# Attention and mixture-of-experts layer on one core: table load, expert parts, projections and plan moved within the steps

## The reference

```python
def attn(x, Wq, bq, Wk, bk, Wv, bv, Wo, bo):        # x: (8, 256, 256), 16 heads of 16
    q, k, v = x @ Wq.T + bq, x @ Wk.T + bk, x @ Wv.T + bv
    phi_q, phi_k = elu(q) + 1, elu(k) + 1
    kv_sum = cumsum(phi_k * v, axis=1)              # along the 256 rows, elementwise
    return (phi_q * kv_sum) * 0.25 @ Wo.T + bo

def ffn(x, router_w, w1, w2, w_gate, w_up, w_down):  # 2048 tokens, 8 experts, top 2
    top, idx = top_k(x @ router_w, 2)
    scores = softmax(top)
    routed = sum over the two experts e of a token:
             score * ((silu(x @ w1[e][:, :512]) * (x @ w1[e][:, 512:])) @ w2[e])
    shared = (silu(x @ w_gate) * (x @ w_up)) @ w_down
    return routed + shared

x = x + attn(layernorm(x), ...)
x = x + ffn(layernorm(x), ...)
```

## Time and profile before

| | before |
|---|---|
| median of 3 runs | 377.15 us (376.57 to 378.16) |
| profiled execution, its own time | 377.39 us |
| its span, first to last instruction | 375.7 us |
| PE busy | 340.8 us (91%) |
| DVE, ACT, POOL busy | 235.5, 214.5, 189.3 us |
| granted TensorE clock, mean | 0.976 |

### The profile page before, as it was taken

The page is one execution under the profiler, slowest core; times in us unless marked ns, Lnnn a source line. Parts: engine busy times, 40 slices in busy tenths (PEclk is TensorE's granted clock), DMA queues, the critical chain, the costliest instruction groups (busy, mean ns, idle before and its releaser), DMA issues.

```text
span 375.7 us, 9015 instructions
## 1 busy us (share of the span) xinstructions
PE 340.8 (91%) x2868; PEld 252.9 (67%) x2868; DVE 235.5 (63%) x579; ACT 214.5 (57%) x385; POOL 189.3 (50%) x293
## 2 busy tenths in 40 slices
PE   7866599999997999999999899999999999999980
PEld 6655488787786878878888555655566566656660
DVE  5977976687766886798677655464544533443430
ACT  3767639666775686876526345544545545455440
POOL 4823085578586775937134532453353534434432
PEclk9998989999998999999999999999999999999995
DMA  7976052337355462464845826647475676695530
GB/s 194 384 190 201 15 130 64 76 91 227 56 149 191 106 198 67 115 199 142 253 154 164 159 54 100 96 70 109 76 111 85 100 101 87 97 109 88 84 49 0
DMA packets 77467, 46.41 MB, mean 124 GB/s; under 512 B 61040, under 2 KB 72560, under 8 KB 77040
## 3 DMA queue, kind: packets, MB, share of 16 engines
q1 hardware_dynamic: 63088, 35.08, 37.0%
q0 software_dynamic: 9664, 10.71, 17.6%
q10 hardware_dynamic: 4672, 0.07, 0.9%
HBM read 19.09 MB, written 12.97 MB: 85 GB/s over the span
## 4 chain that ended last, share of the span: by engine, by line
PE 46%; POOL 18%; DVE 10%; issue 9%; DMA 7%; ACT 7%; POOLq 1%; SPq 1%; DVEq 0%; ACTq 0%
PE bU L1027 13%; PE bG L1027 12%; PE bV L1048 6%; POOL x_rows L570 6%; PE bQ L1048 6%; DMA xs<-bo 3%; PE bK L1007 2%; DMA xT<-rows 2%; PE bU L237 2%; PE bG L237 2%; DVE ab L1475 1%; DMA stage<-in_w_expert 1%; DVE st L1352 1%; POOL y L510 1%; POOL nt L517 1%
## 5 line engine op out<-in xcount | busy, mean ns | idle before, releaser
L1475 DVE SCALAR_TENSOR_TENSOR ab<-bU,sg 128x512 f32<-128x512 f32 x64 | 44.1, 689 | 77.0 <-PE bU L1027 52.2
L761 POOL DMA_INDIRECT out_y<-xs,dst_row x32 | 50.0, 1562 | 60.2 <-DMA out_y<-xs,dst_row 39.2
L1158 ACT ACTIVATE sg<-bG 128x512 f32<-128x512 f32 x64 | 37.9, 593 | 45.4 <-PE bG L1027 26.6
L1027 PE MATMUL bG<-we,work 128*128 (+1 forms) x216 | 52.6, 380 | 1.7 <-DVE wd L1531 1.7
L1027 PE MATMUL bU<-we,work 128*128 (+1 forms) x216 | 52.6, 379 | 0.0
L1302 ACT ACTIVATE ws_h<-ab 128x512 f16<-128x512 f32 x36 | 22.7, 629 | 41.6 <-DVE ab L1475 40.1
L570 POOL DMA_INDIRECT x_rows<-rows,slot_u x32 | 35.1, 1098 | 21.3 <-DVE slot_u L1526 10.7
L1751 DVE TENSOR_TENSOR ws_h<-ab,ws_h 128x512 f16<-128x512 f32 x36 | 25.0, 694 | 20.7 <-ACT ws_h L1302 20.7
L1165 ACT ACTIVATE ah<-ab 128x512 f16<-128x512 f32 x32 | 20.1, 628 | 26.9 <-DVE ab L1475 26.8
L1027 PEld LDWEIGHTS bG<-we,work 128*128 128x128 f16 (+1 forms) x216 | 20.7, 99 | 21.2 <-issue 3.6
L1027 PEld LDWEIGHTS bU<-we,work 128*128 128x128 f16 (+1 forms) x216 | 19.8, 99 | 17.4
(11 more groups left out here) (321 smaller groups left out, 813.8 us busy)
## 6 DMA issues: line engine op xcount, KB each, us to landing
stage<-in_w_expert SPq DMA_DIRECT2D x24, 512.0 KB, 4.6
we<-in_w_shared SPq DMA_DIRECT2D x3, 1024.0 KB, 10.7
xs<-bo POOLq DMA_DIRECT2D x8, 256.0 KB, 3.9
out_y<-xs SPq DMA_DIRECT2D x8, 256.0 KB, 2.5
xs<-in_x SPq DMA_DIRECT2D x1, 1280.0 KB, 19.7
x_rows<-we SPq DMA_DIRECT2D x9, 134.0 KB, 2.4
xs<-in_x SPq DMA_DIRECT2D x3, 256.0 KB, 4.3
work<-x_rows SPq DMA_TRANSPOSE x40, 3.2
```

The lines of the kernel that those rows point to most:

```text
L761: pool.indirect_dma_start(out_rows, bass.IndirectOffsetOnAxis(ap=dst_row[:, b:b + 1], axis=0), ya[b % NY], None, bounds_check=NT * P - 1, ...
L1027: ins = pe.matmul(dst[t * n:(t + 1) * n, :], x2[:, hi * KC + k, t * n:(t + 1) * n], w[t][lo][:, k, half, :], start=s == 0 and k == 0, stop ...
L1158: act.activation(sg[q][:], src[:], ACT.Silu, scale=1.0 / WS).then_inc(S["sg_done"], 1)
L1475: dve.scalar_tensor_tensor(out=ab[q][:], in0=src[:], scalar=1.0 / WS, in1=sg[q][:], op0=ALU.mult, op1=ALU.mult).then_inc(S["a_done"], 1)
```

## The change

All of it is order; besides that, four tiny Exp activations are added.

- **ACT, table.** In steps 3 to 6 a new `load_exp()` (an Exp of one number for each partition, into `spare`) stands behind `silu(n + 3, 1)`, so that the compiler's load of the Exp table stands there and no longer at the head of the next step. `act_hi(j, 3)` goes ahead of `normed2(i)`.
- **ACT and DVE, expert parts.** On ACT the first part of a step goes behind `silu(n, 0)`, the others each one place forward. On DVE steps 3, 5 and 6 take their three parts at the places that steps 4 and 7 already used for their first three (the first one ahead of `swiglu(n + 2, 0)`), and only steps 4 and 7 have one at the end.
- **DVE, second norm.** `logits(i - 1, 2)` goes ahead of `stats2(i)`, `moments2(i)` ahead of `act_lo(j, 1)`.
- **PE.** In steps 3 to 7 Q is projected second and V third. In the last batches `down(B - 2, 0)` goes ahead of `route(B - 1)`, and `spread_plan()` ahead of `gate_up(B - 1, 3)`.
- **Last batches.** Part (B, 2) goes ahead of the plan, the others forward by one place; SP loads part 22 ahead of the clearing of rows; DVE copies the plan's table ahead of part (B, 5); POOL makes the masks ahead of its wait for the token numbers; for block 0 `placed` goes behind `routed_act_lo`.

```diff
 # SP
             load_part(20)
             load_part(21)
+            load_part(22)
...
-            load_part(22)
             load_part(23)
 # PE
-                project(i)
+                project(i, "kqv")
...
             gate_up(B - 2, 1)
+            down(B - 2, 0)
             route(B - 1)
             gate_up(B - 2, 2)
-            down(B - 2, 0)
...
             down(B - 1, 0)
+            spread_plan()
             gate_up(B - 1, 3)
 # ACT
+            def load_exp():
+                act.activation(spare[:], bias[:, 0, 0:1], ACT.Exp)
...
+                first = 0 if i in FOUR else 1
                 exps(i)
                 silu(n, 0)
+                expert_hi(part_of_step(i, first))
                 context_hi(i)
...
                 act_hi(j, 1)
-                if i in FOUR:
-                    expert_hi(part_of_step(i, 0))
-                expert_hi(part_of_step(i, 1))
+                expert_hi(part_of_step(i, first + 1))
                 choice(i - 1)
-                if i not in FOUR:
-                    expert_hi(part_of_step(i, 2))
+                expert_hi(part_of_step(i, first + 2))
                 silu(n + 2, 0)
-                if i in FOUR:
-                    expert_hi(part_of_step(i, 2))
                 act_hi(j, 2)
                 silu(n + 3, 1)
+                if i < B - 1:
+                    load_exp()
+                act_hi(j, 3)
                 normed2(i)
-                act_hi(j, 3)
                 row_hi2(i)
-                expert_hi(part_of_step(i, 3))
+                if i in FOUR:
+                    expert_hi(part_of_step(i, 3))
 # DVE
                 residual(i)
+                logits(i - 1, 2)
                 stats2(i)
-                logits(i - 1, 2)
+                moments2(i)
                 act_lo(j, 1)
-                moments2(i)
                 if ahead:
                     row_lo(0, i + 1)
-                if i in FOUR:
-                    expert_lo(part_of_step(i, 0))
+                first = 0 if i in FOUR else 1
+                expert_lo(part_of_step(i, first))
                 swiglu(n + 2, 0)
-                expert_lo(part_of_step(i, 1))
+                expert_lo(part_of_step(i, first + 1))
                 slots(i - 1, 0)
                 act_lo(j, 2)
                 slots(i - 1, 1)
                 swiglu(n + 3, 1)
-                expert_lo(part_of_step(i, 2))
+                expert_lo(part_of_step(i, first + 2))
                 act_lo(j, 3)
                 row_lo(1, i)
-                expert_lo(part_of_step(i, 3))
+                if i in FOUR:
+                    expert_lo(part_of_step(i, 3))
...
             act_lo(j, 2)
+            expert_lo(part_of_step(B, 2))
             swiglu(n + 3, 1, bV)
```

More of the change, by code:

```diff
@@ L107, in layer_kernel @@
         row_f = sb("row_f", [P, 1])
+        spare = sb("spare", [P, 1])
         xs = sb("xs", [P, NT, D])
@@ L697, in _ @@
                 pool.dma_start(meta[:, b, :], xrows[bass.ds(at, P), 2 * D:2 * D + 8]).then_inc(S[f"first_meta{b}"], 16)
+            pool.wait_ge(S["spread_out"], 2)
+            pool.tensor_copy(pad_i[:, 0:NBLK], past[:, 0:NBLK]).then_inc(S["pad_done"], 1)
+            for t in range(2):
+                then(pool.tensor_scalar(half_pad[:, :, t], mixed_of(past), other[:, t:t + 1], None, ALU.max), wait=t == 1)
+            pool.tensor_copy(half_pad_i[:], half_pad[:]).then_inc(S["pad_done"], 1)
+            then(pool.tensor_tensor(pad_f[:, 1:NBLK], bexp_c[:, 1:NBLK], bexp_c[:, 0:NBLK - 1], ALU.subtract))
+            then(pool.tensor_scalar(pad_f[:, 1:NBLK], pad_f[:, 1:NBLK], 0.0, 16.0, ALU.is_gt, ALU.mult))
             pool.wait_ge(S["spread_in"], 2)
@@ L707, in _ @@
             pool.tensor_scalar(ends[:, 1, :], pick_block[:], tok_f[:, 1:2], None, ALU.mult).then_inc(S["ends_in"], 1)
-            pool.wait_ge(S["spread_out"], 2)
-            pool.tensor_copy(pad_i[:, 0:NBLK], past[:, 0:NBLK]).then_inc(S["pad_done"], 1)
-            for t in range(2):
-                then(pool.tensor_scalar(half_pad[:, :, t], mixed_of(past), other[:, t:t + 1], None, ALU.max), wait=t == 1)
-            pool.tensor_copy(half_pad_i[:], half_pad[:]).then_inc(S["pad_done"], 1)
-            then(pool.tensor_tensor(pad_f[:, 1:NBLK], bexp_c[:, 1:NBLK], bexp_c[:, 0:NBLK - 1], ALU.subtract))
-            then(pool.tensor_scalar(pad_f[:, 1:NBLK], pad_f[:, 1:NBLK], 0.0, 16.0, ALU.is_gt, ALU.mult))
             pool.wait_ge(S["ends_out"], 1)
@@ L792, in project @@
                     pe.wait_ge(S["xT1_in"], 16 * TB * (i - 2))
-                for m, name, done, free in ((0, "k", "k_ps", "rk_done"), (1, "v", "v_ps", "kv_done"), (2, "q", "q_ps", "rq_done")):
-                    if name not in which:
-                        continue
+                parts = {"k": (0, "k_ps", "rk_done"), "v": (1, "v_ps", "kv_done"), "q": (2, "q_ps", "rq_done")}
+                for name in which:
+                    m, done, free = parts[name]
                     if i >= 2:
@@ L1059, in expert @@
                 return pe.snap(expert_reg[b % 3], min_val=0, max_val=E - 1)
-            spread_plan()
             pe.wait_ge(S["bexp_done"], 1)
@@ L1277, in _ @@
             act_hi(j, 2)
+            expert_hi(part_of_step(B, 2))
             silu(n + 3, 1, bK)
@@ L1282, in _ @@
             silu(n, 0)
+            expert_hi(part_of_step(B, 3))
             act_hi(j, 0)
-            expert_hi(part_of_step(B, 2))
             silu(n + 1, 1, bK)
             act_hi(j, 1)
-            expert_hi(part_of_step(B, 3))
+            expert_hi(part_of_step(B, 4))
             silu(n + 2, 0)
-            expert_hi(part_of_step(B, 4))
+            expert_hi(part_of_step(B, 5))
             act_hi(j, 2)
             silu(n + 3, 1, bK)
-            expert_hi(part_of_step(B, 5))
             act_hi(j, 3)
@@ L1733, in _ @@
             act_lo(j, 0)
-            expert_lo(part_of_step(B, 2))
+            expert_lo(part_of_step(B, 3))
             swiglu(n + 1, 1, bV)
             act_lo(j, 1)
-            expert_lo(part_of_step(B, 3))
+            expert_lo(part_of_step(B, 4))
             shared_out(B - 2)
             swiglu(n + 2, 0)
-            expert_lo(part_of_step(B, 4))
+            dve.wait_ge(S["spread_ps"], 1)
+            dve.tensor_copy(bexp_c[:, 0:NBLK], bR[:, 0:NBLK]).then_inc(S["spread_out"], 1)
+            dve.tensor_scalar(past[:, 0:NBLK], bR[:, NBLK:2 * NBLK], row128[:], float(BIG), ALU.is_le, ALU.mult).then_inc(S["spread_out"], 1)
+            expert_lo(part_of_step(B, 5))
             act_lo(j, 2)
             swiglu(n + 3, 1, bV)
-            expert_lo(part_of_step(B, 5))
             act_lo(j, 3)
@@ L1755, in placed @@
                 if k == 0:
+                    if b == 0:
+                        dve.wait_ge(S["spread_out"], 2)
+                        dve.wait_ge(S["pad_done"], 2)
                     dve.wait_ge(*meta_in(b))
@@ L1797, in _ @@
             for b in range(NBLK):
-                placed(b, 0)
+                if b >= 1:
+                    placed(b, 0)
                 swiglu(NP * B + b, b % 2)
-                placed(b, 1)
+                if b >= 1:
+                    placed(b, 1)
                 routed_act_lo(b)
+                if b == 0:
+                    placed(b, 0)
+                    placed(b, 1)
                 if b == 1:
```

5 lines of the change are left out of this document (removed).

## The result

Over six executions each, taken in turn on one chip, the change takes 372.99 us median (372.15 to 373.19) against 376.44 (376.03 to 378.16): ratio 0.9885, 95% interval 0.985 to 0.992, so **3.45 us less**, where 6.15 were forecast (371.0 from 377.15). The profiled execution, the fastest of the six, took 372.15 us, 5.24 less than that of before.

What follows compares the result with a forecast made beforehand. POOL's ring was taken to pace the steps. 377.39 - 4.0 in the laps - 2.3 behind the last lap = 371.1 us for the profiled execution, which is 0.24 above the median, so 371.0 us; range 367.5 to 375.5.

Steps and rivals of the forecast that it cites:

- POOL's ring: Steps 3 to 6: silu(n+1), DVE's work, POOL's norm2, constants, row writes, norm1, then normed1; paces laps of 23.54, 26.06, 23.19 us.
- Moments and `norm2`: Second norm in each step, counted from normed1's start N: moments at N + 5.05, norm2 ending at N + 10.0 us.
- run beside a split end with it: POOL's norm2 beside DVE's splits: operations end with the split; 0 to +0.3 us in three-part steps, -1.8 in step 4.
- Behind the last lap: From the last lap to the first block: PE 1.65 us earlier, last split 2.3 earlier; -2.3 us, bounds 0 and -3.8.
- for `act_hi` ahead of the norm: Behind the last lap: 0.2 us won by act_hi going ahead of the norm, part of PE's 1.65.
- in step 7, which has no `norm1`, there is none: Table load's cover: the ring hides its effect in the laps, nothing does in step 7, so 0.75 us is won there.
- the fourth rival: Table load hidden on ACT was never on the path outside step 7; if step 7 gains nothing, 371.8 us; chance 0.10.
- about 206: Start of the first block in the profile, forecast at about 206 us.
- The rest of a lap: From norm2's end to the next normed1: -0.9, -0.6 and -0.9 us, with norm1 meeting fewer of DVE's operations.
- PE's floor of 22.3 us in a lap: Bank bU, free only at N + 7.9 (N: normed1's start), alone keeps a lap at 22.3 us.
- first rival: Ring gets short enough that every lap is PE's: -7.1 and -2.8, 367.5 us; chance 0.14 for under 368.8.
- The net zero of `ranks` against bU: In the steps PE wins 0.4 to 0.8 us a lap at ranks, loses it waiting for bank bU: net 0.

Runs made afterwards that it cites:

- VectorE's order alone: Kernel before with only the choice and the second norm's moments brought ahead of act_lo(j, 1) on VectorE: 374.94 us, ratio 0.9931.
- steps alone: Kernel before with only the change's hunks in the loop over steps 3 to 7, end as before: 374.86 us, ratio 0.9937.
- the constants away: Changed kernel with POOL's 35 small operations for the plan moved from steps 3 to 6 into step 7: 368.88 us, ratio 0.9764.

## Why the prediction was right, and what was mis-sized

**What bounds the kernel** was read rightly: POOL's ring, not ScalarE's table load, though PE's waits named ACT first. Moving the moments back by 0.6 us cost 6.6 us, taking work out of the ring gives 6.6 us, and with that slack the cost shrinks. The size was read less well. The kernel came out 2.0 us above the 371.0 forecast but gained 2.7 us less; the difference is that before stood at 376.44 beside it and not at 377.15, which is luck.

**Moments and `norm2`:** N + 5.05 and N + 10.0 forecast, N + 5.05 and N + 9.95 measured in all three steps. One reading behind it was loose: of the operations that "run beside a split end with it", the square and `rstd` of step 4 do (102.84 and 105.40 for splits that end at 102.79 and 105.31), the power ends 0.6 us behind its split (101.64 for 101.06).

**Behind the last lap:** -2.3 forecast, -2.2 measured, and the waits named are the ones that went: 0.75 at `gate_up(5, 1)`, 0.70 at `route(7)`, 0.81 of the 1.67 at the first block. The 0.2 us "for `act_hi` ahead of the norm" did not go: PE waits 0.21 us at that `down` as before. And the 0.75 was put down to the table load ("in step 7, which has no `norm1`, there is none"), while the run without the early load has no such wait either: that the load was never on the path, the fourth rival, holds for step 7 too, given that the expert part has left the end of step 6. The first block was to come at "about 206" and came at 207.21, but the loop had started 1.65 us earlier than before; counted from the first `normed1` it came after 138.61 us, where 142.3 - 6.3 = 136.0 were forecast.

**The rest of a lap is the step that failed:** "I take -0.9, -0.6 and -0.9 for the rests", since "`norm1` meets fewer of DVE's operations". Measured, lap less the end of `norm2`, after against before: -0.7, **+1.2** and -0.4. That is 2.5 us of the 2.5 by which the laps missed. In step 4 before, VectorE stood from 105.3 to 107.2 for ACT's `act_hi(j, 3)`, and POOL ran eight constants there at 0.18 to 0.22 us each; one of them and VectorE's wait:

```profile
106.06 0.19 POOL L597 TENSOR_SCALAR mix_at<-half_f 128x4 f32<-128x4 f32 x1
```

```profile
107.24 0.69 DVE L1480 TENSOR_TENSOR al<-ab,ah 128x512 f16<-128x512 f32 x1 [1.93 <-ACT ah L1165]
```

With the change two waits of 0.61 and 0.35 us are left of that gap, and `mix_at` takes 1.14 us and the `mix_thr` behind it 0.63; of the last three, slow before too, one got faster (1.20 to 0.38), and together the constants cost 0.8 us more. The row writes took 1.30, 1.61, 1.07 and 1.49 us for the 1.16, 0.98, 1.37 and 1.07 of before, 0.9 more with what lies between. The loss on the constants doesn't come from the parts or from `act_hi` moved on ACT: VectorE's order alone has it too (5.6 us), since an earlier `norm2` lets `normed2` and `act_hi(j, 3)` start earlier and puts the constants beside VectorE's splits. That on the row writes varies with the rest: 5.7 us in step 4 of "steps alone", whose loop has the same code, 5.2 with VectorE's order alone, 6.4 here. Over the kernel the 32 row writes went from 35.1 to 38.3 us. I had moved VectorE's work earlier and asked only what it leaves, not whom it meets at the new place. Steps 3 and 5 have 8 and 4 constants for the 11 of step 4, and lost less.

**PE's floor of 22.3 us in a lap** from bank bU (first rival) was wrong too: with the constants away PE ran laps of 21.75 and 21.63 us from one `gate_up(j, 2)` to the next, with one wait of 0.65 us at bU in all three.

**The net zero of `ranks` against bU** came out better than said: no wait at `ranks`, and behind `swiglu(n+2)` only one at bU, 0.42 us in step 6.

**What of the change is shown to be worth something:** VectorE's order around the second norm and the end. The table load, the early parts and the order of the projections could each be taken back with a ratio whose interval overlaps the change's.

## What to carry to other kernels

Where a slow engine (here POOL) stands in a ring that passes through a fast one's queue, cost every instruction in its stretch of the ring, also those nobody waits for: 35 small constants that only the end needs were worth more than the whole change. And two engines that hold each other up have no fixed durations: ask of each moved operation which one it will now run beside; 0.6 us later on VectorE cost 1.8 on POOL in `norm2`, and where `norm2` ended earlier the rest of the same lap grew by 1.2.
